# An ODE stage's low-part matmuls on the weights of the high part, with the chunks in three groups

## What is computed

```python
def _mlp(y, W1, b1, W2, b2, W3, b3):
    h = jnp.tanh(y @ W1.T + b1)
    h = jnp.tanh(h @ W2.T + b2)
    return h @ W3.T + b3

def _rk4_step(y, dt, params):
    f = lambda z: _mlp(z, *params)
    k1 = f(y)
    k2 = f(y + dt / 2 * k1)
    k3 = f(y + dt / 2 * k2)
    k4 = f(y + dt * k3)
    return y + dt * (k1 + 2 * k2 + 2 * k3 + k4) / 6
...
    span = 1.0 / (S - 1)
    steps = max(1, int(span / STEP_SIZE))
    dt = span / steps
...
    y0 = x[:, 0]
    _, ys = jax.lax.scan(interval, y0, None, length=S - 1)
```

## Time and profile before

| | before |
|---|---|
| runs, us | 7774.84, 7777.19, 7759.47 (median 7774.84) |
| profiled execution, us | 7759.4 |
| its span, first to last instruction, us | 7757.6 |
| mean granted TensorE clock | 0.566 |
| TensorE matmul busy | 6989.7 us, 90% of the span |
| weight loads busy | 6404.7 us, 83% |
| VectorE busy | 3679.8 us, 47% |
| ScalarE busy | 3037.6 us, 39% |
| GpSimd busy | 1242.1 us, 16% |

### The profile page before, as it was taken

How to read it: one execution, slowest core, us unless ns; L and a number is a source line. 1 busy time by engine, 2 the same in 40 slices (tenths; PEclk the granted TensorE clock), 3 DMA queues, 4 the chain that set the end, 5 groups by cost and what they waited for, 6 DMA issues and landing times. The chain is left out here.

```text
span 7757.6 us, 452418 instructions
## 1 busy us (share of the span) xinstructions
PE 6989.7 (90%) x201621; PEld 6404.7 (83%) x201621; DVE 3679.8 (47%) x16941; ACT 3037.6 (39%) x18260; POOL 1242.1 (16%) x5237
## 2 busy tenths in 40 slices
PE   8884999999999999999999999999999998638886
PEld 3222999999999999999999999999999997426774
DVE  5444444344444444444444444444444444449997
ACT  3331333333333333333333333333333332328886
POOL 1000222112111121122112221122112121010001
PEclk7785555555555555555555555555555555668887
DMA  1000000100010001000100001000100000012332
GB/s 48 1 20 30 5 5 5 43 5 5 5 43 5 5 5 43 5 5 5 43 5 5 5 5 43 5 5 5 43 5 5 5 23 5 0 52 110 119 122 80
DMA packets 45133, 189.84 MB, mean 24 GB/s; under 512 B 7155, under 2 KB 27318, under 8 KB 33030
## 3 DMA queue, kind: packets, MB, share of 16 engines
q1 hardware_dynamic: 38662, 145.18, 4.9%
q0 software_dynamic: 4480, 15.38, 0.6%
HBM read 122.93 MB, written 37.62 MB: 21 GB/s over the span
## 5 line engine op out<-in xcount | busy, mean ns | idle before, releaser
L843 PE MATMUL p<-H,W 128*128 128x4 f16 x130816 | 5336.5, 167 | 77.8 <-issue 32.6
L843 PEld LDWEIGHTS p<-H,W 128*128 128x128 f16 x130816 | 4925.9, 105 | 101.3 <-issue 42.7
L994 DVE TENSOR_TENSOR_SCAN L<-H,h 128x24 f16<-128x24 f16 x8176 | 1689.5, 207 | 3269.9 <-ACT h L926 1914.4
L843 PE MATMUL p<-L,W2D 128*128 128x4 f16 x32704 | 2127.4, 168 | 61.3 <-issue 55.4
L843 PE MATMUL p<-L,W13D 128*128 128x4 f16 x32704 | 2100.6, 168 | 20.3 <-issue 18.2
L843 PEld LDWEIGHTS p<-L,W2D 128*128 128x128 f16 x32704 | 1746.5, 104 | 84.3 <-issue 62.2
L843 PEld LDWEIGHTS p<-L,W13D 128*128 128x128 f16 x32704 | 1731.8, 104 | 35.0 <-issue 26.7
L926 ACT ACTIVATE H<-p 128x8 f16<-128x8 f32 x4088 | 756.0, 185 | 1861.4 <-PE p L843 1861.3
L933 ACT ACTIVATE H<-p 128x8 f16<-128x8 f32 x4088 | 754.4, 185 | 1829.4 <-PE p L843 1754.7
L926 ACT ACTIVATE h<-p 128x8 f32<-128x8 f32 x4088 | 721.4, 177 | 4.4
L933 ACT ACTIVATE h<-p 128x8 f32<-128x8 f32 x4088 | 721.0, 177 | 0.0
(11 more groups left out here) (378 smaller groups left out, 4817.4 us busy)
## 6 DMA issues: line engine op xcount, KB each, us to landing
e_W<-w_scaled SPq DMA_DIRECT2D x23, 2304.0 KB
e_W<-w_scaled SPq DMA_DIRECT2D x23, 1152.0 KB, 5.3
raw_f<-in_spline SPq DMA_DIRECT2D x21, 1024.0 KB, 6.8
w_scaled<-raw_f SPq DMA_DIRECT2D x7, 2304.0 KB, 9.0
w_scaled<-raw_f SPq DMA_DIRECT2D x7, 1152.0 KB, 11.2
raw<-in_spline POOLq DMA_DIRECT2D x3, 1024.0 KB, 6.9
rows_in<-zeros POOLq DMA_DIRECT2D x4, 768.0 KB, 12.0
e_xs<-rows_in SPq DMA_DIRECT2D x12, 256.0 KB, 5.8
```

Source lines behind the costliest of these rows:

```text
L843: ins = pe.matmul(out[:, m, 0:B], weights, x, start=False, stop=(left[m] == 0 and n == len(terms) - 1), skip_group_check=True)
L994: sg.up(dve.tensor_tensor_scan(flat(cols(L, GROUPS[n])), flat(cols(H, GROUPS[n])), flat(cols(h, GROUPS[n])), -1.0, ALU.mult, ALU.add), f"l ...
```

## The change

The low part is no longer scaled by 4096, so it goes through `W[:, 0]` itself; `W2D` and `W13D` and the two casts that make them go. Block terms are now "w" (the second weight part times `H`), "h" (the first part times `H`), "l" (the first part times `L`, with its own load) and "hl" (the first part times `H` and then, on the weights just loaded, times `L`). The second matmul of "hl" is made by `times_loaded`, which issues a matmul with `ldweights=False`. In the table 14 of 16 blocks are "hl"; two keep "h" and "l" apart. The scan goes over two columns per value instead of three. The chunks form three groups, so there are three signals, three pairs of tanh and three scans per product. Ahead of the loop a probe of four such pairs on known numbers is compared with its known sum, and the difference, which is zero when the low part arrives, is added to the bias.

```diff
-    GROUPS = [(0, 1), (2, 3)]
+    GROUPS = [(0,), (1, 2), (3,)]
     G = len(GROUPS)
-    LIFT = 4096.0
-    BLOCKS = [("h", 1, 1), ("h", 1, 2), ("h", 0, 2), ("h", 0, 1), ("h", 1, 0), ("l", 0, 3), ("h", 0, 0), ("l", 1, 0), ("l", 1, 1),
...
+    BLOCKS = [("w", 0, 2), ("h", 0, 3), ("w", 0, 0), ("w", 0, 1), ("w", 0, 3), ("h", 0, 2), ("l", 0, 2), ("hl", 0, 1),
+              ("w", 1, 0), ("w", 2, 0), ("w", 2, 3), ("hl", 0, 0), ("w", 3, 0), ("w", 3, 1), ("w", 2, 1), ("hl", 2, 0),
+              ("hl", 1, 1), ("hl", 1, 0), ("hl", 3, 0), ("w", 1, 1), ("hl", 2, 1), ("hl", 2, 2), ("hl", 3, 1), ("hl", 3, 2),
...
-        W2D, W13D = sb("W2D", [P, KH, HID], F16), sb("W13D", [P, KH, HID], F16)
...
-        H1, H2 = sb("H1", [P, NV, 3], F16), sb("H2", [P, NV, 3], F16)
+        H1, H2 = sb("H1", [P, NV, 2], F16), sb("H2", [P, NV, 2], F16)
...
+        def times_loaded(pe, out, weights, x, stop):
+            return pe.add_instruction(mybir.InstMatmult(
+                name=nc.get_next_instruction_name(), engine=pe.engine, ins=[pe.lower_ap(x), pe.lower_ap(weights)], outs=[pe.lower_ap(out)],
+                start_tensor_calc=False, stop_tensor_calc=stop, tile_size=(P, P), tile_position=(0, 0), bass_skip_group_check=True,
+                ldweights=False))
...
-                terms = [(W[:, q, k, P * m:P * m + P], H[:, columns, 0]) for q in range(NP)] if part == "h" else [
-                    (WD[:, k, P * m:P * m + P], L[:, columns, 1])]
-                for n, (weights, x) in enumerate(terms):
-                    ins = pe.matmul(out[:, m, 0:B], weights, x, start=False, stop=(left[m] == 0 and n == len(terms) - 1), skip_group_check=True)
+                weights = W[:, 1 if part == "w" else 0, k, P * m:P * m + P]
+                x = L if part == "l" else H
+                ins = pe.matmul(out[:, m, 0:B], weights, x[:, columns, 0], start=False, stop=(left[m] == 0 and part != "hl"), skip_group_check=True)
+                if part == "hl":
+                    ins = times_loaded(pe, out[:, m, 0:B], weights, L[:, columns, 0], left[m] == 0)
...
+            sg.wait(pe, "probe", 3)
+            for n in range(4):
+                pe.matmul(pv[:, 0:B], probe_w[:], probe_x[:, 0, :], start=(n == 0), stop=False, skip_group_check=True)
+                ins = times_loaded(pe, pv[:, 0:B], probe_w[:], probe_x[:, 1, :], n == 3)
...
-            for n, (wd, whole) in enumerate(((W2D, W2), (W13D, W13))):
-                sg.wait(act, "part", n + 1)
-                sg.up(act.activation(wd[:], whole[:, 0], ACT.Copy, scale=1.0 / LIFT), "part")
```

More of the change, by code:

```diff
@@ L702, in flow @@
     NV = KH * B
-    GROUPS = [(0, 1), (2, 3)]
+    GROUPS = [(0,), (1, 2), (3,)]
     G = len(GROUPS)
-    LIFT = 4096.0
-    BLOCKS = [("h", 1, 1), ("h", 1, 2), ("h", 0, 2), ("h", 0, 1), ("h", 1, 0), ("l", 0, 3), ("h", 0, 0), ("l", 1, 0), ("l", 1, 1),
[3 rows of a table removed]
+    BLOCKS = [("w", 0, 2), ("h", 0, 3), ("w", 0, 0), ("w", 0, 1), ("w", 0, 3), ("h", 0, 2), ("l", 0, 2), ("hl", 0, 1),
[4 rows of a table added]
+    ALL = 3 * KH
+    PROBE = (2.0 ** -10, 3 * 2.0 ** -24)
     with ExitStack() as ctx:
@@ L719, in flow @@
         sg.add(**{name: UN * k for name, k in step.items()})
-        sg.add(ready=0, turned=0)
+        sg.add(ready=0, turned=0, probe=0, probe_ps=0)
         def wait(eng, name, n, w):
@@ L745, in flow @@
         COEFS = [c * WLOW / WMAX for c in (DT / 2, DT, DT / 6)]
-        H1, H2 = sb("H1", [P, NV, 3], F16), sb("H2", [P, NV, 3], F16)
-        h1, h2 = sb("h1", [P, NV, 3]), sb("h2", [P, 4, NV, 3])
-        L1, L2 = sb("L1", [P, NV, 3], F16), sb("L2", [P, NV, 3], F16)
+        H1, H2 = sb("H1", [P, NV, 2], F16), sb("H2", [P, NV, 2], F16)
+        h1, h2 = sb("h1", [P, NV, 2]), sb("h2", [P, 4, NV, 2])
+        L1, L2 = sb("L1", [P, NV, 2], F16), sb("L2", [P, NV, 2], F16)
+        probe_w, probe_x, counts = sb("probe_w", [P, P], F16), sb("probe_x", [P, 2, B], F16), sb("counts", [P, 1])
         inner, outer, both = sb("inner", [P, NV]), sb("outer", [P, NV]), sb("both", [P, NV])
@@ L785, in _ @@
             for x in (H1, H2):
[L786 to L789, removed]
+                sg.up(pool.memset(x[:, :, 1], 0.0), "zeros")
+            sg.up(pool.memset(h1[:, :, 1], -1.0), "zeros")
             for e in range(4):
-                sg.up(pool.memset(h2[:, e, :, 1], 0.0), "zeros")
-                sg.up(pool.memset(h2[:, e, :, 2], -1.0), "zeros")
+                sg.up(pool.memset(h2[:, e, :, 1], -1.0), "zeros")
             sg.wait(pool, "ones_set", 3)
@@ L824, in _, with product @@
                 pool.drain().then_inc(sg.sem["turned"], 1)
-        def product(pe, w, e, out, W, WD, H, L, high, low, done):
-            left, owed, high_in, low_in = [2 * KH] * KH, list(GROUPS), 0, 0
+        def times_loaded(pe, out, weights, x, stop):
[3 more added lines that the diff above has]
+                ldweights=False))
+        def product(pe, w, e, out, W, H, L, high, low, done):
+            left, owed, high_in, low_in = [ALL] * KH, list(GROUPS), 0, 0
             for part, k, m in BLOCKS:
                 group = next(n for n, q in enumerate(GROUPS) if k in q) + 1
-                if part == "h" and group > high_in:
+                if part != "l" and group > high_in:
                     wait(pe, high, 2 * (G * e + group) - 1, w)
                     high_in = group
-                if part == "l" and group > low_in:
+                if "l" in part and group > low_in:
                     wait(pe, low, G * e + group, w)
                     low_in = group
-                left[m] -= 1
+                left[m] -= len(part)
                 columns = slice(B * k, B * k + B)
-                terms = [(W[:, q, k, P * m:P * m + P], H[:, columns, 0]) for q in range(NP)] if part == "h" else [
-                    (WD[:, k, P * m:P * m + P], L[:, columns, 1])]
-                for n, (weights, x) in enumerate(terms):
-                    ins = pe.matmul(out[:, m, 0:B], weights, x, start=False, stop=(left[m] == 0 and n == len(terms) - 1), skip_group_check=True)
+                weights = W[:, 1 if part == "w" else 0, k, P * m:P * m + P]
[3 more added lines that the diff above has]
+                    ins = times_loaded(pe, out[:, m, 0:B], weights, L[:, columns, 0], left[m] == 0)
                 if owed and all(left[c] == 0 for c in owed[0]):
@@ L868, in _ @@
             sg.up(pe.matmul(py[:, 0:4], t.ones[0:2, :], wdiag[:], start=True, stop=True), "wm_ps")
+            sg.wait(pe, "probe", 3)
+            for n in range(4):
+                pe.matmul(pv[:, 0:B], probe_w[:], probe_x[:, 0, :], start=(n == 0), stop=False, skip_group_check=True)
+                ins = times_loaded(pe, pv[:, 0:B], probe_w[:], probe_x[:, 1, :], n == 3)
+            sg.up(ins, "probe_ps")
             sg.wait(pe, "rest", 2)
@@ L880, in _ @@
                     for e in range(4):
-                        product(pe, w, e, p2, W2, W2D, H1, L1, "h1", "lo1", "u2")
-                        product(pe, w, e, p1, W13, W13D, H2, L2, "h2", "lo2", "u1")
+                        product(pe, w, e, p2, W2, H1, L1, "h1", "lo1", "u2")
+                        product(pe, w, e, p1, W13, H2, L2, "h2", "lo2", "u1")
             pe.wait_ge(sg.sem["turned"], STEPS // UN)
@@ L911, in _ @@
                     sg.up(act.activation(split(q), full, ACT.Copy), "part")
-            for n, (wd, whole) in enumerate(((W2D, W2), (W13D, W13))):
-                sg.wait(act, "part", n + 1)
-                sg.up(act.activation(wd[:], whole[:, 0], ACT.Copy, scale=1.0 / LIFT), "part")
-            sg.wait(act, "zeros", 5 + 2 + 8)
+            sg.wait(act, "zeros", 3 + 1 + 4)
             def steps(scale, factor):
@@ L954, in _ @@
             sg.seq(dve, dve.tensor_copy(wb3[:], pv[:, NV:NV + KH]), "prep")
+            sg.seq(dve, dve.tensor_copy(probe_w[:], t.ones[:]), "probe")
+            for n, x in enumerate(PROBE):
+                sg.seq(dve, dve.tensor_scalar(probe_x[:, n, :], t.ones[:, 0:B], C * x, None, ALU.mult), "probe")
             sg.seq(dve, dve.tensor_scalar(b3dt[:], b3[:], DT, None, ALU.mult), "prep")
@@ L978, in _ @@
             sg.seq(dve, dve.tensor_scalar(mb(b2s[:]), wide(b2[:]), wup[:, 0:1], None, ALU.mult), "prep")
+            sg.wait(dve, "probe_ps", 1)
+            sg.seq(dve, dve.tensor_scalar(counts[:], pv[:, 0:1], 4 * sum(PROBE), 1.0e30 / PROBE[1], ALU.subtract, ALU.mult), "probe")
+            sg.seq(dve, dve.tensor_scalar(b2s[:], b2s[:], counts[:, 0:1], None, ALU.add), "prep")
             for x, n in ((w2f[:], 0), (w13f[:], 1)):
@@ L989, in _ @@
             dve.tensor_copy(sums(p2), mb(b2s[:])).then_inc(sg.sem["ready"], 1)
-            sg.wait(dve, "zeros", 5 + 2 + 8)
+            sg.wait(dve, "zeros", 3 + 1 + 4)
             def low(H, h, L, layer, e, n, w):
```

## The result

| | before | after |
|---|---|---|
| median, us | 7770.24 (four executions, 7759.47 to 7777.19) | 7657.28 (four, 7654.61 to 7662.07) |
| profiled execution: span, us | 7757.6 | 7652.8 |
| matmuls / weight loads in the loop | 196224 / 196224 | 196224 / 138992 |

The ratio is 0.9854, 95% interval 0.9842 to 0.9867: faster by 1.5%, a small gain but clear of the noise. The forecast of 6985 missed by 672 us, and the measured time is 7 us above the range. The case that came is the rival "floor per matmul" (7505 to 7670).

A forecast was written before the change was run, and what follows sets the result against it. It took load-matmul pairs, the tanh-scan chain and the instruction stream as close limits in the ODE step loop; 4088 products x 1.202 us + 75 = 4989 us against 5765, 776 less, so 6985 us, range 6855 to 7650.

The forecast's parts named there:

- floor per matmul: Rival: the 26.7 ns is the matmul's own, load hidden; 1.33 to 1.37 us a product, time 7590; chance 0.18.
- Loads: TensorE, per product: 34 loads at 26.7 ns, 0.907 us, plus 14 load-free matmuls estimated at 4 ns each.
- The chain: Per product, from a group's signal through tanh and scan to its low part: 1.145 us, 1.17 with six load-free matmuls.
- The stream: Instruction fetch by q8 packets: surplus falls from 0.13 to 0.10 us; 3.715 us a packet, 1.202 us a product.
- The scan of 8 elements: First group's scan shrinks from 24 elements to 8: 172 ns in place of 207.
- The seed of p1: Next product's start: seed ready 0.77 us after the second group's tanh, needed after 0.84, so clear by some 0.07 us.
- room: ScalarE's six tanh per product, 0.42 us, and VectorE's one added scan both fit in 1.17 us.
- The time outside the loop: Two casts of 1.89 us go, probe work comes ahead of the loop: difference nothing, 4 us either way.
- Slower: Rival: a load-free matmul holds up the next load by 45 ns; 1.61 us a product, time 8650; chance 0.08.
- no change: Rival: the loads are issued after all, 48 pairs a product, 1.36 to 1.40 us; chance 0.04.
- hidden stream: Rival: instruction fetch costs nothing, the chain alone sets 1.145 to 1.17 us a product, time 6750 to 6850; chance 0.07.

The follow-up runs named there:

- the bursts: Changed kernel plus runs of 32 matmuls ahead of the loop, without loads at 1 to 64 columns and as load-matmul pairs; ran once, 7649.43 us.
- four kernels: Those with 48 loads a product: the kernel before, the changed one with all loads, with the old order and groups, and reordered with all loads; ratios 1, 1.0032, 0.9986, 0.9942.
- 32 columns: Changed kernel reordered to hide waits (37 loads, ratio 0.9466), then each matmul's four columns read eight times: 7190.39 us, ratio 0.9253 to the kernel before.

## Why the prediction was wrong

**The step that failed** is the one headed *Loads*: a matmul without a load at 4 ns, in series. It is 25.0 ns in the bursts and a full slot in the loop. So 34 loads are not 0.907 us with 0.056 behind them, but 48 slots of 26.7, 1.28. Everything after that step fell with it. The chain as summed, with its six load-free matmuls at a slot each, is 1.145 + 6 x 0.0267 = 1.305 us and not 1.17, and TensorE did not wait 0.2 us at the first low part: it doesn't wait there at all. Its 0.09 us stand at the third group's tanh and at that group's low part; the forecast had 0.03 for the scan of that group and nothing for its tanh.

**How the wrong value was chosen.** Its reason was the earlier trace rows, fp32 loads with one and with four columns both at 111 ns a pair. But the matmuls in those rows are fp32 too, so a price per matmul that is the same for one column and four would give the same 111: the rows speak for the load no more than for the matmul. The rival "floor" noted that no f16 row separates them, and then put rows 5 against it. With no row on the quantity that carried 14 x 22.7 ns x 4088 = 1299 us of expected TensorE time, the two ends deserved like weight, and 0.18 for the floor was too little.

**The floor rival** gave 1.33 to 1.37 us a product and 7590; measured are 1.369 and 7657, at its upper end. Its slack for waits, 0.05 to 0.09, was right, at 0.09.

**The stream** was read rightly in kind: the 248 waits and 3.72 us a packet did mean a kernel held at the pace of its instructions (its pauses come by the packet), and with 82 instructions in place of 96 the surplus went, from 0.051 to 0.002 us a product. This is all that the change gained. The forecast left a surplus of 0.10 us a packet only because it put the products at 1.17. The Trainium skill ("Runtime: NRT & Kernel Launch", Instruction fetch mechanics) calls the crossing to a new block mostly hidden; four kernels held at 3.69 to 3.72 us a block disagree, while the kernel after, with 0.002 us a product, agrees.

**Smaller terms.** The scan of 8 elements was put at 172 ns and measures 175. The seed of p1 was rightly named as late next, but its slack of 0.07 us does not exist: ScalarE waits 892.9 us for it. It is not among TensorE's 0.09 us, which are the same in both layers. ScalarE and VectorE did have room (50% and 55% busy). The time outside the loop fell by 105 - 101 = 4 us, inside the 4 allowed.

**Slower, no change, hidden stream.** A load-free matmul does not run together with the next load, but neither does it hold it up by 45 ns: from the matmul ahead of it to the one behind it is 0.05 us on the timeline, two slots. The loads really went (138992). In the kernel after the stream is hidden, as the last rival has it, but that rival's time goes by the chain at 4 ns and falls with it.

**Left open.** What sets 3.7 us for a packet was not tried, only that no kernel's stretch here goes below it. The transfer itself is not it: 1.9% of 16 engines' 580 us, over 156 packets, is 1.13 us a packet. Nor why 32 columns raise the granted clock and four don't.

## What to carry to other kernels

Ask of each instruction that a change removes whether it occupies a slot of its own: with small matmuls the matmul does and its load hides behind it, so count matmuls, not loads. When no row separates two costs that always come together, measure the one alone, a burst of 32 on known numbers is enough, before an order is built on a guess. And look at the instruction queue: when several kernels of one instruction count take the same time per packet, instructions are the currency, and removing hidden ones pays only up to the next limit, which here is the order's waits.

## What was not expected of the hardware

A matmul without a load costs 25 ns for 1, 4 or 16 columns at 1.2 GHz, and a pair with four columns the same at 2.4 GHz. The stream of instructions held four kernels at 3.69 to 3.72 us a packet. And 28 useless columns made the loop faster: the granted clock went from 0.50 to 0.97 over the loop, and the ratio to before from 0.9466 to 0.9253.
